# Three full score passes in place of two stacked passes and a pair of 33-row strips, in the third of four attentions

## The chip, the cores and the metric

The kernel runs on one core of one Trainium2 chip. The metric is the time of one execution on the device, in microseconds (us). TensorE, VectorE, ScalarE and GpSimd (PE, DVE, ACT and POOL in the profile) run side by side and wait for one another by semaphores; SyncE (SP) issues DMAs.

## The reference

Eight sequences of 256 tokens (2048 rows of 128) go through four layers, each a gated cross attention and a gated feed-forward part. The third attention (`_L2_xattn_ref`) has 8 heads, and its head split folds the sequences into the rows:

```python
def _split_heads(t):
    b, n, _ = t.shape
    t = t.reshape(b, n, HEADS, DIM_HEAD)
    return t.transpose(2, 0, 1, 3).reshape(HEADS, b * n, DIM_HEAD)
sim = jnp.einsum('hid,hjd->hij', qh, kh) * SCALE
mean = jnp.mean(sim, axis=-1, keepdims=True)
sim = (sim - mean) * ATTN_MATRIX_SCALE + mean
attn = jax.nn.softmax(sim, axis=-1)
out = jnp.einsum('hij,hjd->hid', attn, vh)
```

So every query meets all 2048 keys, in each of 8 heads. x has 128 features and the context has 96.

## The kernel before

The weights of queries and keys are folded into one 128 x 96 matrix for each head, so a query is a vector of 96 that is multiplied with the context itself. Numbers are split into two 16-bit halves, high and low, and a product of two split numbers is made of three 16-bit products: high by high, high by low, low by high. The context lies in `M.ct_hi` (97 rows, the 97th all ones) and `M.ct_lo` (96 rows), each with 2048 keys.

`attention_wide` works through 32 blocks (8 heads by 4 groups of 512 queries), each of 8 units of 256 keys. The order of the work is written out by hand, one list for each engine, and a wait on a semaphore stands ahead of each step. For block b and unit u (n = 8b + u) TensorE does:
- `max_scores(b + 2, 2u)` (L1245): scores in high halves alone, for a block two later, 512 keys at a time. Their row maximum is subtracted later. It writes the one bank MAXB, which VectorE's reduction (L1452, `largest`) has to have read.
- `scores(n + 2)` (L1272, L1273, L1277): the scores of a unit two later, keys on the partitions, 512 queries in each of two banks.
- `max_scores(b + 2, 2u + 1)`.
- `weighted(n)` (L1294, L1297): 16 products of p's halves with the context.
- at u = 1 `max_row(b + 1)` (L1255: turns the negated maxima into a row), at u = 2 `turn` (L1308), at u = 3 `query(b + 3)` (L1229 to L1231), at u = 5 `project` (L1316).

ScalarE does `exps(n + 2)`: the exponent twice, to `p` in 32 bits (L1368) and to its high half `p_hi` (L1370), and copies the high half of the query (L1354), the row of maxima (L1358), the first half of the sums (L1378). The low half `p_lo` = p - p_hi is made in two halves, one by VectorE (L1464) and one by GpSimd (L1416). VectorE's order in a unit is: reduction 2u (L1452), p_lo of unit n + 1 (L1464), reduction 2u + 1; at u = 0 ahead of these the second half of the sums (`u_second`, L1471), at u = 3 behind them the low half of the query (L1443), at u = 5 and 6 the addition to x (L1486), at u = 7 the maximum over keys (L1458). GpSimd does p_lo's other half, and at u = 0 a sum (L1424).

The products of the scores have 96 + 96 + 97 rows to be contracted, 289 together. Before, they are stacked: K1 and K2 hold 128 rows of keys each, K3 the last 32 and a row of ones, at partitions 0 and 64; S1, S2 and S3 hold the query rows that belong to them. The key stacks are made once, and the query stacks by five DMAs a block on SyncE's queue (`stack`, `double`). Two full passes with 128 rows each and a third with 33 rows make a bank's scores; the third ones of the two banks lie in different row groups of the array and run side by side.

Of the kernel before, what the change touches and what calls it, by code (L numbers as in the profile page):

```python
# [21 lines left out]
F16 = mybir.dt.float16  # L22
BF16 = mybir.dt.bfloat16
ALU = mybir.AluOpType
ACT = mybir.ActivationFunctionType
# [3 lines left out]
P = 128  # L29
D = 128  # L30
DC = 96
DA = DC + 1
NTOK = 2048
NT = NTOK // P
QB = 512
# [1097 lines left out]
def attention_wide(nc, M, layer):  # L1133
    L = LAYERS[layer]
    NB = L.H * NQ
    UQ = NT // 2
    NU = NB * UQ
    JOB, MAXB, UB = 6, 7, 4
    VW = DA + 1
    MAXS = NT  # L1140
    ps, A_hi, A_lo, C = M.ps, M.A_hi[layer], M.A_lo[layer], M.C[layer]

    with ExitStack() as ctx:
        def sb(name, shape, dt):
            return ctx.enter_context(nc.sbuf_tensor(f"aw_{name}", shape, dt))

        def sem(name):
            sems.append(nc.alloc_semaphore(f"aw_{name}"))
            return sems[-1]

        sems = []

        K1, K2, K3 = (sb(f"keys{i}", [P, NTOK], F16) for i in range(3))
        S1, S2, S3 = (sb(f"queries{i}", [P, 4, QB], F16) for i in range(3))
        QL = sb("q_lo", [DC, 2, QB], F16)
        p = sb("p", [P, 2, 2 * QB], F32)
        p_hi = sb("p_hi", [P, 3, 2 * QB], F16)
        p_lo = sb("p_lo", [P, 3, 2 * QB], F16)
# [4 lines left out]
        UT = sb("u_turned", [DC, 2, QB], F32)  # L1163
        rden = sb("rden", [P, 2, TQ, 1], F32)

        ones_set, keys_loaded = sem("ones_set"), sem("keys_loaded")
        q_ready, qhi_done, q_done = sem("q_ready"), sem("q_hi_done"), sem("q_lo_done")
        stacked = [sem(f"stacked{i}") for i in range(4)]
        doubled = [sem(f"doubled{i}") for i in range(4)]
        m_ready, m_done, n_done = sem("max_scores_ready"), sem("max_done"), sem("neg_max_done")  # L1170
        r_ready, r_done = sem("max_row_ready"), sem("max_row_done")
        st_ready, p_done, hi_done = sem("scores_ready"), sem("p_done"), sem("p_hi_done")
# [5 lines left out]
        def is_block(b):  # L1178
            return 0 <= b < NB

        def is_unit(n):
            return 0 <= n < NU

        with nc.Block() as block:
            @block.sync
            def _(sp):
                sp.dma_start(K1[0:DC, :], M.ct_hi[0:DC, :]).then_inc(keys_loaded, 16)
                sp.dma_start(K1[DC:P, :], M.ct_hi[0:32, :]).then_inc(keys_loaded, 16)
                sp.dma_start(K2[0:64, :], M.ct_hi[32:DC, :]).then_inc(keys_loaded, 16)
                sp.dma_start(K2[64:P, :], M.ct_lo[0:64, :]).then_inc(keys_loaded, 16)  # L1190
                for r in (0, 64):
                    sp.dma_start(K3[r:r + 32, :], M.ct_lo[64:DC, :]).then_inc(keys_loaded, 16)

                def stack(b):
                    c = b % 4
                    sp.wait_ge(qhi_done, b + 1)
                    sp.dma_start(S2[64:P, c, :], S1[0:64, c, :]).then_inc(stacked[c], 16)
                    sp.dma_start(S3[0:32, c, :], S1[64:DC, c, :]).then_inc(stacked[c], 16)
                    sp.wait_ge(q_done, b + 1)
                    sp.dma_start(S1[DC:P, c, :], QL[0:32, b % 2, :]).then_inc(stacked[c], 16)  # L1200
                    sp.dma_start(S2[0:64, c, :], QL[32:DC, b % 2, :]).then_inc(stacked[c], 16)

                def double(b):
                    c = b % 4
                    sp.wait_ge(stacked[c], 64 * (b // 4 + 1))
                    sp.wait_ge(r_done, b + 1)
                    sp.dma_start(S3[64:97, c, :], S3[0:33, c, :]).then_inc(doubled[c], 16)

                for b in range(3):
                    stack(b)  # L1210
                double(0)
                for b in range(NB):
                    if is_block(b + 1):
                        double(b + 1)
                    if is_block(b + 3):
                        stack(b + 3)

            @block.tensor
            def _(pe):
                def query(b):  # L1220
# [12 lines left out]
                def max_scores(b, k):  # L1233
                    t, kb = divmod(k, NQ)
                    if k == 0:
                        pe.wait_ge(qhi_done, b + 1)
                    step = MAXS * b + k
                    bank = MAXB
                    if b < 2:
                        bank = (UB + 1, MAXB)[k % 2]  # L1240
                        if step >= 2:
                            pe.wait_ge(m_done, step - 1)
                    else:
                        pe.wait_ge(m_done, step)
                    nc.tensor.matmul(ps[:, bank, :], S1[0:DC, b % 4, t * P:(t + 1) * P],  # L1245
                                     M.ct_hi[0:DC, kb * QB:(kb + 1) * QB], start=True, stop=True
                                     ).then_inc(m_ready, 1)

# [10 lines left out]
                def scores(n):  # L1259
                    b, u = divmod(n, UQ)  # L1260
                    c = b % 4
                    if n == 0:
                        pe.wait_ge(keys_loaded, 6 * 16)
                        pe.wait_ge(ones_set, 2)
                    if u == 0:
                        pe.wait_ge(stacked[c], 64 * (b // 4 + 1))
                        pe.wait_ge(doubled[c], 16 * (b // 4 + 1))
                    if n >= 2:
                        pe.wait_ge(hi_done, n - 1)
                    for i in range(2):  # L1270
                        o, ks = ps[:, 2 * (n % 2) + i, :], slice((2 * u + i) * P, (2 * u + i + 1) * P)
                        nc.tensor.matmul(o, K1[:, ks], S1[:, c, :], start=True, stop=False)  # L1272
                        nc.tensor.matmul(o, K2[:, ks], S2[:, c, :], start=False, stop=False)  # L1273
                    for i in range(2):
                        o, ks = ps[:, 2 * (n % 2) + i, :], slice((2 * u + i) * P, (2 * u + i + 1) * P)
                        rows = slice(64 * i, 64 * i + 33)
                        ins = nc.tensor.matmul(o, K3[rows, ks], S3[rows, c, :], start=False, stop=True)  # L1277
                    ins.then_inc(st_ready, 1)

                def weighted(n):  # L1280
# [48 lines left out]
                for b in range(NB):  # L1329
                    for u in range(UQ):  # L1330
                        n = UQ * b + u
# [19 lines left out]
            def _(act):  # L1351
                def query(b):
                    act.wait_ge(q_ready, b + 1)
                    nc.scalar.activation(S1[0:DC, b % 4, :], ps[0:DC, JOB, :], ACT.Copy).then_inc(qhi_done, 1)  # L1354

                def max_row(b):
                    act.wait_ge(r_ready, b + 1)
                    nc.scalar.activation(S3[32:33, b % 4, :], ps[0:1, JOB, :], ACT.Copy).then_inc(r_done, 1)  # L1358

                def exps(n):  # L1360
                    act.wait_ge(st_ready, n + 1)
# [26 lines left out]
                for b in range(3):  # L1388
                    query(b)
# [3 lines left out]
                for b in range(NB):  # L1393
                    for u in range(UQ):
                        n = UQ * b + u
# [11 lines left out]

            @block.gpsimd
            def _(pool):
                for r in (32, 96):  # L1410
                    nc.gpsimd.memset(K3[r:r + 1, :], 1.0).then_inc(ones_set, 1)

                def lows(n):
                    pool.wait_ge(hi_done, n + 1)
                    pool.wait_ge(p_done, n + 1)
                    nc.gpsimd.tensor_tensor(p_lo[:, n % 3, QB:], p[:, n % 2, QB:], p_hi[:, n % 3, QB:],  # L1416
                                            ALU.subtract).then_inc(lo_b, 1)

                def u_sum(b):
                    pool.wait_ge(ue_a, b + 1)  # L1420
                    pool.wait_ge(ue_b, b + 1)
                    if b >= 2:
                        pool.wait_ge(t_ready, b - 1)
                    nc.gpsimd.tensor_tensor(us[:, b % 2], UE[:, b % 2, :, 0:DC], UE[:, b % 2, :, VW:VW + DC], ALU.add  # L1424
                                            ).then_inc(us_done, 1)

                lows(0)
                for b in range(NB):
                    for u in range(UQ):
                        n = UQ * b + u  # L1430
                        if is_unit(n + 1):
                            lows(n + 1)
                        if u == 0 and is_block(b - 1):
                            u_sum(b - 1)
                u_sum(NB - 1)

            @block.vector
            def _(dve):
                def query(b):
                    dve.wait_ge(qhi_done, b + 1)  # L1440
                    if b >= 2:
                        dve.wait_ge(stacked[(b - 2) % 4], 64 * ((b - 2) // 4 + 1))
                    nc.vector.tensor_tensor(QL[:, b % 2, :], ps[0:DC, JOB, :], S1[0:DC, b % 4, :], ALU.subtract  # L1443
                                            ).then_inc(q_done, 1)

                def largest(b, k):
# [44 lines left out]
                for b in range(3):  # L1491
                    query(b)
# [5 lines left out]
                for b in range(NB):  # L1498
                    for u in range(UQ):
                        n = UQ * b + u  # L1500
# [707 lines left out]
```

## Time and profile before

| what | value |
|---|---|
| median of 3 runs | 2666.34 us (2664.91 to 2668.88) |
| the profiled execution's own time | 2664.91 us |
| its span, first to last instruction | 2662.8 us |
| mean granted TensorE clock | 0.922 |
| TensorE, VectorE, ScalarE, GpSimd busy | 2293.9, 1955.0, 1518.6, 517.3 us |
| third attention, first to last product starts | 1047.6 to 1896.9 us |

Busy time is the time in which an engine has an instruction under way. Products overlap in the pipeline: a product of 512 columns is shown 0.38 us long, and the next one starts 0.22 us after it. What a product costs its engine is read from start to start.

### The profile page before, as it was taken

To read this page: it belongs to the slowest core of one execution; us is meant where nothing else is said; L and a number is where in the kernel's file an instruction comes from. 1 tells how busy PE (TensorE), PEld (TensorE's weight loads), DVE (VectorE), ACT (ScalarE), POOL (GpSimd) and SP (SyncE) were. 2 spreads that over 40 slices of the span, in tenths; PEclk is the share of its full clock that TensorE was granted. 3 is DMA by queue.
4 is the path that set the end of the run, shared out by engine and by line. 5 is a ranking of instruction groups with operands and counts; after the bars stand their busy time and mean duration, and the time that the engine had idled before them with its cause. 6 is when DMAs were issued, how large, how long until landed. Compare 5 with 4: busy or idle time off the path is not lost. (4 is left out here: it accounts for less than half of the span.)

```text
span 2662.8 us, 53217 instructions
## 1 busy us (share of the span) xinstructions
PE 2293.9 (86%) x19264; PEld 1535.1 (58%) x19265; DVE 1955.0 (73%) x3972; ACT 1518.6 (57%) x2054; POOL 517.3 (19%) x451
## 2 busy tenths in 40 slices
PE   3699439999969996999999999999679959999777
PEld 3444227888746663455555555555456638888644
DVE  2566457888858886787787877877447758888778
ACT  1257206777635552566666666667468837777511
POOL 2100010000022221343443444444322110000000
PEclk9679669999979997899999999999789969999889
DMA  5001100000010001000000000000010000000000
GB/s 141 0 6 10 19 0 1 0 0 0 1 48 25 24 1 30 8 9 11 11 9 12 9 11 9 11 12 6 1 41 24 1 1 1 0 0 0 1 17 26
DMA packets 68181, 35.68 MB, mean 13 GB/s; under 512 B 40939, under 2 KB 63699, under 8 KB 67670
## 3 DMA queue, kind: packets, MB, share of 16 engines
q1 hardware_dynamic: 63412, 30.84, 4.8%
q10 hardware_dynamic: 4610, 2.71, 0.4%
q8 instruction: 101, 1.65, 0.2%
q14 instruction: 58, 0.48, 0.1%
HBM read 22.75 MB, written 2.10 MB: 9 GB/s over the span
## 5 line engine op out<-in xcount | busy, mean ns | idle before, releaser
L1368 ACT ACTIVATE aw_p<-ps 128x1024 f32<-128x1024 f32 x256 | 262.3, 1024 | 259.8 <-PE ps L1277 259.8
L1452 DVE TENSOR_REDUCE aw_max_part<-ps 128x1 f32<-128x512 f32 x512 | 349.8, 686 | 76.6 <-PE ps L1245 74.1
L1416 POOL TENSOR_TENSOR aw_p_lo<-aw_p,aw_p_hi 128x512 f16<-128x512 f32 x256 | 303.1, 1184 | 498.7 <-ACT aw_p_hi L1370 498.6
L1294 PE MATMUL ps<-ctx_hi_lo,aw_p_hi 128*128 128x194 f16 x2048 | 290.8, 247 | 1.1 <-DVE aw_p_lo L1464 0.7
L1464 DVE TENSOR_TENSOR aw_p_lo<-aw_p,aw_p_hi 128x512 f16<-128x512 f32 x256 | 267.3, 1044 | 22.4 <-ACT aw_p_hi L1370 22.4
L1297 PE MATMUL ps<-ctx_hi_lo,aw_p_lo 128*128 128x97 f16 x2048 | 279.4, 207 | 0.0
L1370 ACT ACTIVATE aw_p_hi<-ps 128x1024 f16<-128x1024 f32 x256 | 260.5, 1018 | 0.0
L428 POOL TENSOR_TENSOR ln_rstd<-ln_var_eps,neg_half 128x16 f32<-128x16 f32 x8 | 23.3, 2918 | 1129.3 <-DVE ln_var_eps L414 1094.8
L2095 DVE TENSOR_TENSOR ex_hidden_lo<-ex_hidden,ex_hidden_hi 128x512 f16<-128x512 f32 x256 | 195.3, 765 | 64.0 <-ACT ex_hidden L2052 63.7
L1245 PE MATMUL ps<-ctxT_hi,aw_queries 96*128 96x512 f16 x512 | 204.1, 400 | 35.8 <-DVE aw_max_part L1452 35.1
L1297 PEld LDWEIGHTS ps<-ctx_hi_lo,aw_p_lo 128*128 128x128 f16 x2048 | 200.3, 98 | 26.0
L2041 ACT ACTIVATE ex_silu<-ps 128x512 f32<-128x512 f32 x164 | 97.9, 597 | 191.6 <-PE ps L1981 189.3
L1977 PE MATMUL ps<-x_normT_hi,ex_w_hi 128*128 128x512 f16 x456 | 175.6, 385 | 34.6 <-POOL ex_w_lo L1942 34.3
L1294 PEld LDWEIGHTS ps<-ctx_hi_lo,aw_p_hi 128*128 128x128 f16 x2048 | 199.7, 97 | 4.8 <-issue 3.7
L1272 PE MATMUL ps<-aw_queries,aw_keys 128*128 128x512 f16 x512 | 194.9, 381 | 0.0
L1273 PE MATMUL ps<-aw_queries,aw_keys 128*128 128x512 f16 x512 | 194.4, 380 | 0.0
L2008 PE MATMUL ps<-ex_w_hi,ex_hidden_hi 128*128 128x128 f16 x1024 | 176.3, 220 | 20.3 <-DVE ex_hidden_lo L2095 16.6
L1010 ACT ACTIVATE at_p<-ps 128x1024 f32<-128x1024 f32 x128 | 131.1, 1024 | 102.6 <-PE ps L916 102.6
L1068 DVE TENSOR_REDUCE at_neg_max<-ps 128x2 f16<-128x512 f32 x256 | 174.3, 681 | 6.0 <-PE ps L895 5.6
L2104 DVE SCALAR_TENSOR_TENSOR x_res<-ps,comb,x_res 128x128 f32<-128x128 f32 x544 | 152.6, 343 | 35.5 <-PE ps L2012 30.1
L2012 PE MATMUL ps<-ex_w_hi,ex_hidden_lo 128*128 128x128 f16 x1024 | 176.3, 220 | 0.0
L2010 PE MATMUL ps<-ex_w_lo,ex_hidden_hi 128*128 128x128 f16 x1024 | 176.3, 220 | 0.0
(288 smaller groups left out, 5716.7 us busy)
## 6 DMA issues: line engine op xcount, KB each, us to landing
ex_w_raw<-in_L_w SPq DMA_DIRECT2D x8, 512.0 KB, 3.3
ex_w<-in_L_w SPq DMA_DIRECT2D x16, 256.0 KB, 2.8
aw_queries<-aw_queries SPq DMA_DIRECT2D x32, 64.0 KB, 2.0
aw_queries<-aw_q_lo SPq DMA_DIRECT2D x32, 64.0 KB, 2.0
ex_w_raw<-in_L_w SPq DMA_DIRECT2D x8, 256.0 KB, 2.6
raw<-in_L_q SPq DMA_DIRECT2D x3, 512.0 KB, 11.0
raw<-in_L_o SPq DMA_DIRECT2D x3, 512.0 KB, 12.8
raw<-in_L_k SPq DMA_DIRECT2D x3, 384.0 KB, 7.6
```

Of the source, the lines that this page charges most:

```text
L1245: nc.tensor.matmul(ps[:, bank, :], S1[0:DC, b % 4, t * P:(t + 1) * P], M.ct_hi[0:DC, kb * QB:(kb + 1) * QB], start=True, stop=True).then_i ...
L1272: nc.tensor.matmul(o, K1[:, ks], S1[:, c, :], start=True, stop=False)
L1273: nc.tensor.matmul(o, K2[:, ks], S2[:, c, :], start=False, stop=False)
L1294: nc.tensor.matmul(ps[:, bank, at:at + 2 * VW - 2], p_hi[:, n % 3, cols], M.cv[:, kt, 0:2 * VW - 2], start=kt == 0 and t % 2 == 0, stop=False,
L1297: ins = nc.tensor.matmul(ps[:, bank, at:at + DA], p_lo[:, n % 3, cols], M.cv[:, kt, 0:DA], start=False, stop=kt == NT - 1, skip_group_chec ...
L1368: nc.scalar.activation(p[:, n % 2, :].rearrange("p (b q) -> p b q", b=2), s, ACT.Exp, scale=1.0 / QS).then_inc(p_done, 1)
L1370: nc.scalar.activation(p_hi[:, n % 3, :].rearrange("p (b q) -> p b q", b=2), s, ACT.Exp, scale=1.0 / QS).then_inc(hi_done, 1)
L1416: nc.gpsimd.tensor_tensor(p_lo[:, n % 3, QB:], p[:, n % 2, QB:], p_hi[:, n % 3, QB:], ALU.subtract).then_inc(lo_b, 1)
L1452: nc.vector.tensor_reduce(mpart[:, b % 2, k:k + 1], ps[:, bank, :], AX.X, ALU.max).then_inc(m_done, 1)
L1464: nc.vector.tensor_tensor(p_lo[:, n % 3, 0:QB], p[:, n % 2, 0:QB], p_hi[:, n % 3, 0:QB], ALU.subtract).then_inc(lo_a, 1)
L2008: nc.tensor.matmul(o, hid_hi[b][:, f, tok], w2_hi[j][:, f, :], start=f == 0, stop=False)
L2095: nc.vector.tensor_tensor(hid_lo[q % 2][:, f, :], hid1[f % 2][:], hid_hi[q % 2][:, f, :], ALU.subtract).then_inc(hid_done, 1)
```

## The change

The stacks, the DMAs that fill them, the memsets and ten semaphores go. The scores read the context as it lies, and the query's halves from `q_hi` (97 rows: the 97th is the row of negated maxima, which ScalarE writes) and `q_lo` (96 rows), both with room for four blocks. A bank's scores are three passes: high keys with high queries (97 rows), low keys with high queries (96), high keys with low queries (96). So a unit has six products of 128 x 512 as before, but none of them run side by side.

```diff
-        K1, K2, K3 = (sb(f"keys{i}", [P, NTOK], F16) for i in range(3))
-        S1, S2, S3 = (sb(f"queries{i}", [P, 4, QB], F16) for i in range(3))
-        QL = sb("q_lo", [DC, 2, QB], F16)
+        q_hi = sb("q_hi", [DA, 4, QB], F16)
+        q_lo = sb("q_lo", [DC, 4, QB], F16)
...
-            @block.sync
-            def _(sp):
-                sp.dma_start(K1[0:DC, :], M.ct_hi[0:DC, :]).then_inc(keys_loaded, 16)
...
-                def stack(b):
-                    c = b % 4
-                    sp.wait_ge(qhi_done, b + 1)
-                    sp.dma_start(S2[64:P, c, :], S1[0:64, c, :]).then_inc(stacked[c], 16)
-                    sp.dma_start(S3[0:32, c, :], S1[64:DC, c, :]).then_inc(stacked[c], 16)
-                    sp.wait_ge(q_done, b + 1)
-                    sp.dma_start(S1[DC:P, c, :], QL[0:32, b % 2, :]).then_inc(stacked[c], 16)
-                    sp.dma_start(S2[0:64, c, :], QL[32:DC, b % 2, :]).then_inc(stacked[c], 16)
-
-                def double(b):
-                    c = b % 4
-                    sp.wait_ge(stacked[c], 64 * (b // 4 + 1))
-                    sp.wait_ge(r_done, b + 1)
-                    sp.dma_start(S3[64:97, c, :], S3[0:33, c, :]).then_inc(doubled[c], 16)
...
-                    if n == 0:
-                        pe.wait_ge(keys_loaded, 6 * 16)
-                        pe.wait_ge(ones_set, 2)
                     if u == 0:
-                        pe.wait_ge(stacked[c], 64 * (b // 4 + 1))
-                        pe.wait_ge(doubled[c], 16 * (b // 4 + 1))
+                        pe.wait_ge(q_done, b + 1)
+                        pe.wait_ge(r_done, b + 1)
                     if n >= 2:
                         pe.wait_ge(hi_done, n - 1)
                     for i in range(2):
                         o, ks = ps[:, 2 * (n % 2) + i, :], slice((2 * u + i) * P, (2 * u + i + 1) * P)
-                        nc.tensor.matmul(o, K1[:, ks], S1[:, c, :], start=True, stop=False)
-                        nc.tensor.matmul(o, K2[:, ks], S2[:, c, :], start=False, stop=False)
-                    for i in range(2):
-                        o, ks = ps[:, 2 * (n % 2) + i, :], slice((2 * u + i) * P, (2 * u + i + 1) * P)
-                        rows = slice(64 * i, 64 * i + 33)
-                        ins = nc.tensor.matmul(o, K3[rows, ks], S3[rows, c, :], start=False, stop=True)
+                        nc.tensor.matmul(o, M.ct_hi[:, ks], q_hi[:, c, :], start=True, stop=False)
+                        nc.tensor.matmul(o, M.ct_lo[:, ks], q_hi[0:DC, c, :], start=False, stop=False)
+                        ins = nc.tensor.matmul(o, M.ct_hi[0:DC, ks], q_lo[:, c, :], start=False, stop=True)
                     ins.then_inc(st_ready, 1)
...
-                    if b >= 2:
-                        dve.wait_ge(stacked[(b - 2) % 4], 64 * ((b - 2) // 4 + 1))
```

## Rows read from the trace of the kernel before

**Rows 1.** The page: busy time, share of the span and instructions of each engine.
```profile
PE 2293.9 (86%) x19264; PEld 1535.1 (58%) x19265; DVE 1955.0 (73%) x3972; ACT 1518.6 (57%) x2054; POOL 517.3 (19%) x451
```
**Rows 2.** Busy time by stretch: us, engines' busy us and instructions, granted clock, DMA.
```profile
1079.20:1084.00 4.80, 4.80 (x13) 1.20 (x12) 1.44 (x4) 1.94 (x2) 0.06 (x1) 0.52 0.00 0
1084.00:1887.60 803.60, 771.86 (x6624) 465.39 (x6623) 628.38 (x975) 553.48 (x630) 338.95 (x285) 1.00 0.04 10
```
**Rows 3.** Waits, 1300 to 1500 us: us in total, times, longest.
```profile
PE ps L1245 <- DVE aw_max_part L1452: 8.2, 16, 0.6
```
**Rows 4.** TensorE in order of time: start, length, instruction, idle before it.
```profile
1415.11 0.38 PE L1245 MATMUL ps<-ctxT_hi,aw_queries 96*128 96x512 f16 x1
1415.33 0.38 PE L1272 MATMUL ps<-aw_queries,aw_keys 128*128 128x512 f16 x1
...
1415.98 0.38 PE L1273 MATMUL ps<-aw_queries,aw_keys 128*128 128x512 f16 x1
1416.29 0.39 PE L1277 MATMUL ps<-aw_queries,aw_keys 33*128 33x512 f16 x2
1416.61 0.39 PE L1245 MATMUL ps<-ctxT_hi,aw_queries 96*128 96x512 f16 x1
...
1418.45 0.38 PE L1245 MATMUL ps<-ctxT_hi,aw_queries 96*128 96x512 f16 x1 [0.43 <-DVE aw_max_part L1452]
...
1424.02 0.38 PE L1255 MATMUL ps<-ident,aw_neg_max 128*1 128x128 f16 x4
1424.43 0.39 PE L1245 MATMUL ps<-ctxT_hi,aw_queries 96*128 96x512 f16 x1
```
**Rows 5.** TensorE around the query products of two blocks.
```profile
1405.05 0.38 PE L1231 MATMUL ps<-x_normT_hi,A_lo 128*96 128x512 f16 x1
1405.26 0.38 PE L1245 MATMUL ps<-ctxT_hi,aw_queries 96*128 96x512 f16 x1
...
1407.43 0.39 PE L1245 MATMUL ps<-ctxT_hi,aw_queries 96*128 96x512 f16 x1 [0.60 <-DVE aw_max_part L1452]
...
1430.80 0.38 PE L1231 MATMUL ps<-x_normT_hi,A_lo 128*96 128x512 f16 x1
```
**Rows 6.** VectorE in order of time, units u7 and u1.
```profile
1415.53 0.69 DVE L1452 TENSOR_REDUCE aw_max_part<-ps 128x1 f32<-128x512 f32 x1
1416.14 1.56 DVE L1464 TENSOR_TENSOR aw_p_lo<-aw_p,aw_p_hi 128x512 f16<-128x512 f32 x1
1417.62 0.68 DVE L1452 TENSOR_REDUCE aw_max_part<-ps 128x1 f32<-128x512 f32 x1
...
1422.21 1.56 DVE L1464 TENSOR_TENSOR aw_p_lo<-aw_p,aw_p_hi 128x512 f16<-128x512 f32 x1
1423.69 0.68 DVE L1452 TENSOR_REDUCE aw_max_part<-ps 128x1 f32<-128x512 f32 x1
```
**Rows 7.** GpSimd in order of time, the same units.
```profile
1416.00 1.16 POOL L1416 TENSOR_TENSOR aw_p_lo<-aw_p,aw_p_hi 128x512 f16<-128x512 f32 x1 [2.55 <-ACT aw_p_hi L1370]
...
1422.07 1.16 POOL L1416 TENSOR_TENSOR aw_p_lo<-aw_p,aw_p_hi 128x512 f16<-128x512 f32 x1 [0.89 <-ACT aw_p_hi L1370]
```
**Rows 8.** ScalarE in order of time, units u4, u6 and u7.
```profile
1405.46 0.59 ACT L1354 ACTIVATE aw_queries<-ps 96x512 f16<-96x512 f32 x1
...
1414.90 1.02 ACT L1370 ACTIVATE aw_p_hi<-ps 128x1024 f16<-128x1024 f32 x1
1416.72 1.02 ACT L1368 ACTIVATE aw_p<-ps 128x1024 f32<-128x1024 f32 x1 [0.80 <-PE ps L1277]
```
**Rows 9.** VectorE and GpSimd, released by the same copy, first p_lo of the stage.
```profile
1083.90 0.69 DVE L1464 TENSOR_TENSOR aw_p_lo<-aw_p,aw_p_hi 128x512 f16<-128x512 f32 x1 [3.33 <-ACT aw_p_hi L1370]
1083.94 1.66 POOL L1416 TENSOR_TENSOR aw_p_lo<-aw_p,aw_p_hi 128x512 f16<-128x512 f32 x1 [32.77 <-ACT aw_p_hi L1370]
```
**Rows 10.** ScalarE and VectorE at the start: the third query's copy and low half.
```profile
1054.93 0.59 ACT L1354 ACTIVATE aw_queries<-ps 96x512 f16<-96x512 f32 x1 [2.33 <-PE ps L1231]
...
1056.26 0.69 DVE L1443 TENSOR_TENSOR aw_q_lo<-ps,aw_queries 96x512 f16<-96x512 f32 x1 [2.94 <-DMA aw_queries<-aw_q_lo]
```

## What is predicted, and why

> **What bounds the kernel now.** I read the page first: TensorE is busy 86% of the span, more than any other engine [rows 1]. The change touches one stage only, so I then took the table by stretches. The third attention's steady part, 1084.0 to 1887.6 us, is 803.6 us in which TensorE is busy 771.9 us (96%) at granted clock 1.00; VectorE has 628.4, ScalarE 553.5 and GpSimd 339.0 [rows 2]. The chain of work that ended last names 2% of the span and helps nothing here, so I took the waits: in 200 us TensorE waits for VectorE's max reductions (L1452) 16 times, 8.2 us [rows 3]. Four per cent idle is little, but it sits always in the same places, and the change can move it.
>
> The next view is TensorE in order of time. One block (512 queries of one head, eight units of 256 keys) takes 25.75 us, by the same L1231 in two blocks (1405.05 and 1430.80) [rows 5]. Call the units u0 to u7. In a unit the order is first max product, scores, second max product, weighted sums. TensorE is back to back except at three places of a block:
> - second max product of u4 (1407.43): 0.60 idle, behind the query product's copy on ScalarE and its low half on VectorE [rows 5].
> - first max product of u0 (1418.45): 0.43 idle; by the steps of the weighted sums it would have come at about 1417.85 [rows 4].
> - first max product of u2 (1424.43): it comes 0.41 after the four L1255 products began, 0.74 after the reduction at 1423.69 began, as the one at 1407.43 comes 0.74 after its own [rows 4, 6]; the four products alone need about 0.31 (an estimate from the smallest such distance read in the stage), so about 0.1 is wait.
>
> Why is VectorE late there? At u7 its p_lo subtraction (L1464) takes 1.56 us where one alone takes 0.69 [rows 9], because GpSimd's half of the same work began 0.14 us before it (1416.00 against 1416.14) and runs until 1417.16. VectorE then ends 0.54 after GpSimd, at 1417.70; the reduction follows at 1417.62 (a VectorE instruction starts some 0.08 before the last one's end) and TensorE at 1418.45. At u1 it is the same: 1422.07 against 1422.21, 1.56 long, reduction at 1423.69 [rows 6, 7]. I counted 57 such collisions of 0.14 to 0.15 us among the 256 subtractions, two in nearly every block; the block of 25.75 repeats with a tick of 0.01. Where VectorE is first by 0.04 it takes 0.69 and GpSimd 1.66 instead of 1.16 [rows 9]. So who comes first decides, and the second waits.
>
> **TensorE's work.** Old scores of a unit: three steps of a full pass (1415.33 to 1415.98, 0.217 each), 0.31 to the pair of 33-row products, 0.32 from the pair to the next product, 1.28 together (1415.33 to 1416.61) [rows 4]. New: six full passes. The rows hold passes of 96 rows next to passes of 128 with the usual step (128 to 96: 1405.05 to 1405.26; 96 to 128: 1415.11 to 1415.33) [rows 4, 5], so 97 and 96 rows should step alike: 6 x 0.2165 = 1.30. The difference is +0.01 to +0.02 a unit; I take 0.015. So the pair, though it runs at once, cost 0.415 net of everything, nearly two passes: what its concurrency gains, the 0.095 ahead of it and the 0.105 behind it take away.
>
> The skill bears on both halves. The Trainium skill, "TensorEngine Tiling (Array Packing)", section Theoretical Speedup, promises up to 2x for contractions of at most 64 rows, and its Key Properties say that changing the tiling mode drains the engine. The trace agrees with both together: 0.31 and 0.32 around the pair instead of 0.22. By the first alone the pair would be worth one pass and the change would cost 0.2165 x 256 = 55 us; by row it is 4.
>
> **When scores are ready.** This term matters more. ScalarE's exponent starts 1.39 after the first score pass (1415.33 to 1416.72) [rows 4, 8]. New: 5 x 0.2165 to the start of the sixth pass and 0.42 to its reader (as 1415.11 to 1415.53) [rows 4, 6] = 1.50. So ScalarE, and behind it GpSimd (its subtraction starts 1.10 after L1370 does, 1414.90 to 1416.00 [rows 7, 8]), come 0.10 to 0.11 later against TensorE; I take 0.105. Most of it is hidden: weighted sums use these values two units later. It is not hidden where GpSimd's end holds VectorE and VectorE's reduction holds TensorE: u7 (scores of u6) and u1 (scores of u0).
>
> Walk a block from the query product Q (L1231 group) of u3. The wait at u4 starts from the query product and absorbs that unit's 0.015; ScalarE must be free for the copy (1405.46 [rows 8]); it would be 0.09 later and was free some 0.14 early (an estimate from back-to-back steps of 0.92 behind the exponent), so it stays free. u5 adds 0.015 until u6's scores start, then 0.105 through exponent, GpSimd, p_lo, reduction, first max of u0: +0.12 instead of +0.045. From there scores of u0 start, 0.105 again through GpSimd of u1 to the first max of u2; then u2 and u3 add 0.03: +0.135. A block: +0.255. TensorE's own 0.015 in u6, u7, u0, u1 vanishes in the two waits. Of 32 blocks 30 run beside max products, and the first of them settles in: 29 x 0.255 = +7.4 us. The last two blocks have no max products and TensorE sets their pace: 16 x 0.015 = +0.2, and the last exponent +0.1.
>
> **Does the collision keep its order?** Against TensorE, GpSimd comes 0.105 later and VectorE's p_lo (behind the unit's first max) 0.015. Its lead of 0.14 becomes 0.05. Observed: GpSimd ahead by 0.14 wins, VectorE ahead by 0.04 wins [rows 6, 7, 9]; 0.05 lies between. I take GpSimd first, since in both rows the earlier starter won.
> The Trainium skill, "SBUF — State Buffer", section SBUF: two separate sides, has it that whichever starts first keeps the shared port pair for its whole instruction. The trace agrees at both leads seen; by that rule 0.05 is enough and the sum stands.
>
> **What is removed elsewhere.** The DMAs: SyncE's queue only issued them; nobody but the first score pass and q_lo waited. In the steady state the waits of TensorE are those on VectorE [rows 3] and none for a DMA, so they give nothing; without that cover nothing is lost either, as q_done and r_done lie units before. The new waits for these stand ahead of a block's first scores, with the unit's second max and weighted sums queued behind. At the start VectorE's third q_lo waits 2.94 us for a DMA (1056.26) where its input was ready at about 1055.55 (copy 1054.93 plus 0.59, plus 0.04) [rows 10]: -0.7, handed on through the paced max products. There the first two units' scores run at a granted clock of 0.52 (1.2 GHz), 13 products in 4.8 us [rows 2]; a pass steps twice as long, and twelve passes take 12 x 0.43 = 5.1 against about 4.6 us as read: +0.5. Net -0.2 (bounds -0.7 and +0.1). The memsets (GpSimd) and ten fewer semaphores to clear lie where GpSimd has nothing to do: 0.
>
> **Sum.** 7.4 + 0.2 + 0.1 - 0.2 = +7.5 us on the profiled execution's 2664.91 (span 2662.8) = 2672.4. The median of before is 1.4 higher, 2666.34: so **2673.8 us**.
>
> **Rivals.**
> 1. VectorE gets the pair first at u7 (lead 0.05 not enough). Then p_lo of u7 takes 0.68, the u0 wait of 0.6 goes, and GpSimd ends 0.5 late. But the exponent of u7's scores is not earlier: it starts at Q+12.24 (Q the query product's start, by the steps above), and GpSimd's next subtraction 0.92 + 1.10 later, Q+14.26. VectorE's p_lo of u0 comes at Q+14.6 (weighted sums readable 13.50, u_second copy 0.51, reduction 0.60), so GpSimd is first, VectorE ends at 14.26 + 1.16 + 0.54 = 15.96, its second reduction starts at 15.89, and the first max of u1 0.74 later, Q+16.63. Before, that point was Q+16.57. The 0.55 gained is given back in the next unit; u1's collision then is 0.6 apart, the u2 wait goes, and the block ends at 25.77 against 25.75. Total about +0.5: 2666.8. For it: 0.05 is a third of the lead seen. Chance 0.27.
> 2. Faster: as 1, but u0 does not give it back. That needs VectorE's p_lo of u0 ahead of GpSimd's, which is 0.35 earlier there; from that point on 0.55 less 0.05 a block is kept: 29 x 0.5 = -14.5, 2652. Against it: both engines' starts hang on rows that don't move so far. Chance 0.06.
> 3. The 0.2 around the pair isn't a switch and stays with the neighbours: scores cost 6 x 0.2165 + 0.2, TensorE +0.215 x 256 = +55 less absorbed waits (1.3 a block, part of it): 2700 to 2722. Against: the plain passes on either side step 0.22. Chance 0.04.
> 4. GpSimd first, as forecast: 0.55. The rest, 0.08, is for what I don't see.
>
> **Numbers.** 0.2% is 5.3 us, about what a measurement of this kernel tells from no change. Case 4 lies at 2673.8 +- 3, five sixths of it beyond +5.3 us; case 1 within. Slower 0.54, same 0.37, faster 0.09. Range: from 2663 (case 1 less run spread of 2 and a start gain) to 2678 (+0.11 and +0.02 taken everywhere, 29 x 0.29, plus spread): 2663 to 2678; the likeliest case alone 2670.5 to 2677.
>
> **What would show it.** Score passes stepping 0.22 with 1.30 to the second max; exponent 1.50 behind the first pass; block 26.0 us (case 4) or 25.75 to 25.8 (case 1); p_lo of u7 and u1 still 1.56 with GpSimd 0.05 ahead, or 0.68 with GpSimd 1.66; waits of TensorE at u0 about 0.7 and at u2 0.2; no DMA wait at the start. Wrong if the 97-row and 96-row passes don't alternate at 0.22, if a 0.05 lead behaves otherwise, or if a later stage shifts by itself.

## The result

Eight runs of each kernel: 2674.98 us after (2671.06 to 2676.51) against 2667.82 us before (2664.91 to 2670.49), a ratio of 1.0026 with a 95% interval of 1.0016 to 1.0037. The change costs about 7.2 us (4.3 to 9.9 by the interval). The forecast was +7.5 us, a median of 2673.8 us. The median of the kernel before is 2667.82 over eight runs and was 2666.34 over the three that the forecast started from.

The page of the kernel after, busy time, share of the span and instructions (before: [rows 1]), and under it the table of its steady stretch (before: [rows 2]):

```profile
PE 2298.9 (86%) x19264; PEld 1578.0 (59%) x19265; DVE 1965.2 (74%) x3972; ACT 1516.2 (57%) x2054; POOL 512.5 (19%) x449
```
```profile
1084.00:1894.00 810.00, 776.87 (x6622) 506.87 (x6621) 636.59 (x971) 550.52 (x628) 336.22 (x284) 1.00 0.01 1
```

The numbers of instructions on PE are the same, so the form of a block is what has to be compared. Line numbers have moved: L1272 and L1273 are now L1232 and L1233, the 33-row L1277 is a full pass L1234, the max product L1245 is L1208, p_lo L1464 and L1416 are L1416 (DVE) and L1370 (POOL). TensorE after, in order of time, units u7, u0 and u1 (before: [rows 4]):

```profile
1413.64 0.38 PE L1208 MATMUL ps<-ctxT_hi,aw_q_hi 96*128 96x512 f16 x1
1413.86 0.38 PE L1232 MATMUL ps<-aw_q_hi,ctxT_hi 97*128 97x512 f16 x1
...
1414.95 0.38 PE L1234 MATMUL ps<-aw_q_lo,ctxT_hi 96*128 96x512 f16 x1
1415.17 0.38 PE L1208 MATMUL ps<-ctxT_hi,aw_q_hi 96*128 96x512 f16 x1
1417.08 0.38 PE L1208 MATMUL ps<-ctxT_hi,aw_q_hi 96*128 96x512 f16 x1 [0.52 <-DVE aw_max_part L1404]
...
1422.67 0.38 PE L1218 MATMUL ps<-ident,aw_neg_max 128*1 128x128 f16 x4
1423.17 0.39 PE L1208 MATMUL ps<-ctxT_hi,aw_q_hi 96*128 96x512 f16 x1
```

Six full passes take 1.31 (1413.86 to 1415.17), where the rows showed 1.28 before; over 240 units of each trace, start to start, the medians are 1.304 and 1.282. The step behind the second max product goes the other way: 0.215 after a stretch of full passes, 0.226 after the strips. A unit of TensorE's work has grown by 0.011 net. The wait at u0 is 0.52 and was 0.43; the one at u2 shows as 0.50 from the four L1218 products to the max product and was 0.41. VectorE and GpSimd in the same units (before: [rows 6, 7]):

```profile
1414.67 1.66 DVE L1416 TENSOR_TENSOR aw_p_lo<-aw_p,aw_p_hi 128x512 f16<-128x512 f32 x1
1416.25 0.68 DVE L1404 TENSOR_REDUCE aw_max_part<-ps 128x1 f32<-128x512 f32 x1
...
1420.85 1.66 DVE L1416 TENSOR_TENSOR aw_p_lo<-aw_p,aw_p_hi 128x512 f16<-128x512 f32 x1
1422.43 0.68 DVE L1404 TENSOR_REDUCE aw_max_part<-ps 128x1 f32<-128x512 f32 x1
```
```profile
1414.63 1.15 POOL L1370 TENSOR_TENSOR aw_p_lo<-aw_p,aw_p_hi 128x512 f16<-128x512 f32 x1 [2.56 <-ACT aw_p_hi L1327]
...
1420.81 1.15 POOL L1370 TENSOR_TENSOR aw_p_lo<-aw_p,aw_p_hi 128x512 f16<-128x512 f32 x1 [1.00 <-ACT aw_p_hi L1327]
```

GpSimd is first by 0.04 now and was by 0.14, and still has its 1.15 us undisturbed, while VectorE's 1.56 became 1.66. ScalarE's exponent follows the first pass by 1.51 (1413.86 to 1415.37 below) where it was 1.39 [rows 4, 8]; over the stage the medians are 1.50 and 1.39:

```profile
1415.37 1.02 ACT L1325 ACTIVATE aw_p<-ps 128x1024 f32<-128x1024 f32 x1 [0.81 <-PE ps L1234]
```

And the block, by the query product's third part in two blocks (before 25.75: [rows 5]), with the wait at u4 between:

```profile
1403.55 0.38 PE L1194 MATMUL ps<-x_normT_hi,A_lo 128*96 128x512 f16 x1
...
1405.94 0.39 PE L1208 MATMUL ps<-ctxT_hi,aw_q_hi 96*128 96x512 f16 x1 [0.48 <-DVE aw_max_part L1404]
...
1429.56 0.38 PE L1194 MATMUL ps<-x_normT_hi,A_lo 128*96 128x512 f16 x1
```

A block takes 26.01 us. The product at u4 comes 2.39 behind the query product's third part and came 2.38 behind it [rows 5], so that unit's part is absorbed, as the walk had it. The wait for the DMA at the start is gone, -0.71: first query product to first score pass is 31.87 us before (1047.56 to 1079.43) and 31.16 after (1042.96 to 1074.12).

**Where the profiled 6.2 us are** (2671.06 against 2664.91). The instruction L428 of each layer norm marks the stages. The third attention with the norm behind it, from its fifth to its sixth, is 868.3 us before (1035.5 to 1903.8) and 877.7 after (1030.9 to 1908.6), +9.4. Of these, 28 blocks from the first query product in the loop to the last are 720.41 and 727.52, +7.1; the start is +0.05 (the wait for the DMA -0.71; the twelve passes of the first two units, which run at half clock, +0.51, from 4.61 to 5.12; the first partial block +0.25); the units behind the last query product are +0.8. The last 1.4 belong to the clock: the last turn and projection took 0.64 and 1.16 us before, and 1.09 and 2.08 after, at a granted clock of 0.50 (1.2 GHz). Of the eleven profiles only this one of the kernel before has the projection at 1.16; in the other ten it takes 2.07 or 2.08, also in e4 and e8, which are built on the kernel before. The turn is 0.64 in e1, e3 and e8 and 0.96 to 1.09 in the others. So the projection's 0.9 us are scatter and not the change's; for the turn's 0.45 it stays open. Outside this stage the profiled run was 4.6 us ahead before it began and lost 1.4 behind it; the same instructions run there, and I come back to that scatter below.

### The profile page after: what moved, and what is told of

The parts are those of the page before. It is cut to its first block and busy times, and to the rows that moved or that the text cites. A ratio compares the mean times of both kernels' runs of the same rounds, so it can differ in the third digit from the quotient of the medians.

```text
span 2668.9 us, 52976 instructions
## 1 busy us (share of the span) xinstructions
PE 2298.9 (86%) x19264; PEld 1578.0 (59%) x19265; DVE 1965.2 (74%) x3972; ACT 1516.2 (57%) x2054; POOL 512.5 (19%) x449
## 2 busy tenths in 40 slices
DMA packets 58163, 26.97 MB, mean 10 GB/s; under 512 B 38443, under 2 KB 54003, under 8 KB 57654
## 3 DMA queue, kind: packets, MB, share of 16 engines
q8 instruction: 101, 1.65, 0.3%
## 5 line engine op out<-in xcount | busy, mean ns | idle before, releaser
L1370 POOL TENSOR_TENSOR aw_p_lo<-aw_p,aw_p_hi 128x512 f16<-128x512 f32 x256 | 302.3, 1181 | 511.6 <-ACT aw_p_hi L1327 511.4
L1416 DVE TENSOR_TENSOR aw_p_lo<-aw_p,aw_p_hi 128x512 f16<-128x512 f32 x256 | 280.5, 1096 | 23.1 <-ACT aw_p_hi L1327 23.1
L428 POOL TENSOR_TENSOR ln_rstd<-ln_var_eps,neg_half 128x16 f32<-128x16 f32 x8 | 23.3, 2916 | 1126.1 <-DVE ln_var_eps L414 1091.8
L1208 PE MATMUL ps<-ctxT_hi,aw_q_hi 96*128 96x512 f16 x512 | 201.6, 395 | 37.0 <-DVE aw_max_part L1404 33.8
L1232 PE MATMUL ps<-aw_q_hi,ctxT_hi 97*128 97x512 f16 x512 | 195.4, 382 | 0.0
L1233 PE MATMUL ps<-aw_q_hi,ctxT_lo 96*128 96x512 f16 x512 | 195.2, 381 | 0.0
L1234 PE MATMUL ps<-aw_q_lo,ctxT_hi 96*128 96x512 f16 x512 | 194.1, 379 | 0.0
```

Source lines behind the costliest of these rows:

```text
L1208: nc.tensor.matmul(ps[:, bank, :], q_hi[0:DC, b % 4, t * P:(t + 1) * P], M.ct_hi[0:DC, kb * QB:(kb + 1) * QB], start=True, stop=True).then ...
L1232: nc.tensor.matmul(o, M.ct_hi[:, ks], q_hi[:, c, :], start=True, stop=False)
L1233: nc.tensor.matmul(o, M.ct_lo[:, ks], q_hi[0:DC, c, :], start=False, stop=False)
L1416: nc.vector.tensor_tensor(p_lo[:, n % 3, 0:QB], p[:, n % 2, 0:QB], p_hi[:, n % 3, 0:QB], ALU.subtract).then_inc(lo_a, 1)
```

## The experiments

All are compared with the kernel before on the same chip; the ratio and its interval are to that kernel. "Block" is the period in the steady part, "stage" the distance between the same two norms' L428 in the profiled run.

| kernel | block us | stage us | median us | ratio to before, 95% interval |
|---|---|---|---|---|
| before | 25.75 | 868.3 | 2664 to 2668 in the sets | 1 |
| after | 26.01 | 877.7 | 2674.98 | 1.0026 (1.0016 to 1.0037) |
| e1 strips on plain halves | 25.785 | 872.5 | 2667.19 | 1.0010 (1.0001 to 1.0019) |
| e2 shorter exponent | 25.79 | 870.9 | 2667.70 | 1.0012 (1.0003 to 1.0020) |
| e3 VectorE first, changed kernel | 25.165 | 852.6 | 2650.67 | 0.9946 (0.9933 to 0.9959) |
| e4 VectorE first, kernel before | 25.09 | 850.6 | 2644.58 | 0.9922 (0.9907 to 0.9938) |
| e5 VectorE first at u7 | 25.75 | 870.2 | 2666.80 | 1.0004 (0.9994 to 1.0015) |
| e6 VectorE first at u7, u0 | 25.165 | 853.6 | 2650.38 | 0.9939 (0.9925 to 0.9952) |
| e7 strips one after the other | 26.97 | 912.1 | 2710.15 | 1.0169 (1.0151 to 1.0187) |
| e8 both moves, kernel before | 24.43 | 830.5 | 2627.93 | 0.9852 (0.9838 to 0.9865) |
| e9 both moves, changed kernel | 24.51 | 833.9 | 2632.40 | 0.9860 (0.9842 to 0.9878) |

**e1: strips without stacks and DMAs.** Did the stacks and their DMAs cost the old kernel anything, or is its time that of its order of passes?

```diff
-                        ins = nc.tensor.matmul(o, M.ct_hi[0:DC, ks], q_lo[:, c, :], start=False, stop=True)
+                    for i in range(2):
+                        o, ks = ps[:, 2 * (n % 2) + i, :], slice((2 * u + i) * P, (2 * u + i + 1) * P)
+                        rows = slice(64 * i, 64 * i + 33)
+                        ins = nc.tensor.matmul(o, M.ct_hi[rows, ks], q_hi[rows, c, :], start=False, stop=True)
```

> The changed kernel, but each bank's third pass is a 33-row strip again (rows 0 to 32 and 64 to 96 of the plain halves, side by side), without stacks and DMAs; this leaves out most of the third product's rows and adds others. Theory A (the time comes from TensorE's order of passes and from when the scores are ready, nothing from the DMAs): block 25.75 us, time that of the kernel before, less up to 0.7 at the start: 0 to -1 us. Rival B (the stacks' DMAs, or 128 rows against 97, cost the old kernel something in the steady state): the block is shorter than 25.75 and the time below before by more than 3 us.

The block is 25.785, within 0.03 of before's: the steps around the pair are the old 0.31 and 0.32, the wait at u0 the old 0.6, and no DMA runs. So the DMAs cost the old steady state nothing, and rival B fell. The rows account for the 0.03: the second and third steps between e1's full passes are 0.218 and 0.218 where the kernel before has 0.215 and 0.215, 0.007 a unit by the medians (1.289 against 1.282). The walk of the prediction has five units on the path (u5, u6, u0, u2, u3), which makes 0.035. Why the steps differ no run shows. The time is 2.7 us above before (interval 0.3 to 5), where 0 to -1 was expected: a miss. In the profiled run the loop has 0.9 us more than before. The stretch from the first query product to the loop has 2.2 more (50.9 us against 48.7 in both other kernels); its last 15 us (1077.6 to 1092.6) had a granted clock of 0.75, where the kernel before had 1.00 from 1084.0 on [rows 2]. Behind the last query product there are 1.1 more, 0.9 of them in the same projection at half clock. So some 3 of the 4.2 us by which the stage is longer are the clock's in this one profile; whether the other runs share it stays open.

**e2: the exponent shortened by what the scores come late.** The test that tells readiness from pass time:

```diff
-                    nc.scalar.activation(p[:, n % 2, :].rearrange("p (b q) -> p b q", b=2), s, ACT.Exp,
+                    w = QB if n < 2 else QB - 64
+                    nc.scalar.activation(p[:, n % 2, :].rearrange("p (b q) -> p b q", b=2)[:, :, 0:w], s[:, :, 0:w],
+                                         ACT.Exp, scale=1.0 / QS).then_inc(p_done, 1)
```

> The changed kernel with ScalarE's first exponent over 448 instead of 512 columns of each bank from the third unit on (it leaves out an eighth of p): some 0.107 us shorter, so GpSimd's subtraction begins again when it did before, while TensorE's six passes stay. Theory A (late readiness of the scores, through ScalarE, GpSimd, VectorE, holds TensorE at u0 and u2): block 26.01 - 2 x 0.107 = 25.80, GpSimd 0.15 ahead at u7 and u1 again, time about 6 us below the changed kernel, 1 to 2 above before. Rival C (TensorE's longer score passes are the cost; ScalarE is idle a third of the time): no change, block 26.0, 7 us above before.

TensorE's passes are those of the changed kernel, and ScalarE has 0.10 us less to do (its first exponent is 0.92 long where it was 1.02). Query products stand at 1403.69 and 1429.48. GpSimd, VectorE and TensorE in turn:

```profile
1415.09 1.15 POOL L1371 TENSOR_TENSOR aw_p_lo<-aw_p,aw_p_hi 128x512 f16<-128x512 f32 x1 [2.56 <-ACT aw_p_hi L1328]
```
```profile
1415.24 1.55 DVE L1417 TENSOR_TENSOR aw_p_lo<-aw_p,aw_p_hi 128x512 f16<-128x512 f32 x1
1416.72 0.68 DVE L1405 TENSOR_REDUCE aw_max_part<-ps 128x1 f32<-128x512 f32 x1
...
```
```profile
1403.69 0.38 PE L1192 MATMUL ps<-x_normT_hi,A_hi 128*96 128x512 f16 x1
...
1429.48 0.38 PE L1192 MATMUL ps<-x_normT_hi,A_hi 128*96 128x512 f16 x1
```

The lead is 0.15 again, VectorE's subtraction 1.55, the block 25.79. Of the 0.255 that the change adds to a block, 0.22 are late readiness on an engine that is idle a third of the time, and 0.04 TensorE's own. Rival C fell.

**e3 and e4: VectorE's half always first.** One wait in GpSimd's list, on the changed kernel and on the one before:

```diff
                     pool.wait_ge(p_done, n + 1)
+                    pool.wait_ge(lo_a, n + 1)
                     nc.gpsimd.tensor_tensor(p_lo[:, n % 3, QB:], p[:, n % 2, QB:], p_hi[:, n % 3, QB:],
```

> The changed kernel with one more wait: GpSimd's half of each p_lo starts only when VectorE's half is done. Theory A: the 1.66 us subtractions at u7 and u1 become 0.68, TensorE's waits at u0 (0.69) and u2 (0.18) go, only that at u4 (0.64) stays: block 25.15, 25 us below the changed kernel, 18 below before. Rival 1 of the prediction in its general form (the gain is given back in the next unit, since the exponents are no earlier): block 25.7 to 25.8, about the time of before. Rival D (GpSimd's half now comes too late for the weighted sums): slower than the changed kernel.

> The kernel before with the same one wait. Theory A: block 25.75 - 0.60 - 0.10 = 25.05 us, some 20 us below before; against the same wait on the changed kernel only TensorE's own difference of 8 x 0.0125 = 0.1 a block is left, 3 us instead of 7. Rival C (the difference of 7 us is TensorE's passes): the two stay 7 us apart.

VectorE, GpSimd and TensorE of e3 at u7 and u0:

```profile
1432.55 0.68 DVE L1417 TENSOR_TENSOR aw_p_lo<-aw_p,aw_p_hi 128x512 f16<-128x512 f32 x1
1433.46 0.69 DVE L1405 TENSOR_REDUCE aw_max_part<-ps 128x1 f32<-128x512 f32 x1 [0.23 <-PE ps L1208]
```
```profile
1433.40 1.16 POOL L1371 TENSOR_TENSOR aw_p_lo<-aw_p,aw_p_hi 128x512 f16<-128x512 f32 x1 [1.29 <-DVE aw_p_lo L1417]
```
```profile
1434.30 0.38 PE L1208 MATMUL ps<-ctxT_hi,aw_q_hi 96*128 96x512 f16 x1
```

The subtraction takes 0.68, the reduction waits for TensorE and no more the other way, and the first max product of u0 has no wait. Blocks are 25.165 and 25.09, as expected within 0.04, so neither is the gain given back nor does GpSimd's half come too late. The blocks differ by 0.075, where 8 x 0.0125 = 0.1 was expected, and the two stages by 2.0 us. Their medians differ by 6, and I put no weight on that: e4's six runs fall into three at 2641.1 to 2642.0, with a mean granted clock of 0.922 to 0.924, and three at 2647.2 to 2647.4, with 0.918 to 0.920. Against the kernel before, e3 is 14 us faster and e4 20, by the medians. Against the kernel that each is built on, the added wait saved about 21 us both times, an estimate from the ratios (1.0026 to 0.9946, and 1 to 0.9922).

**e5 and e6: VectorE first in single units.** The same wait, under `if n % UQ == 0` (u7's) and `if n % UQ in (0, 1)` (u7's and u0's), on the changed kernel. e5 is rival 1 of the prediction, built.

> The changed kernel, GpSimd waiting for VectorE's half only for the p_lo made in u7. Theory A with the prediction's rival 1 as a mechanism: at u0 the first max product comes without a wait, but GpSimd's next subtraction is then ahead of VectorE's (about 0.35), VectorE ends late and the first max product of u1 waits some 0.6; the wait at u2 goes. Block 25.79, 6 us below the changed kernel, about 0 to 1 above before. Theory E (a collision avoided is a collision saved): 0.7 a block kept, block 25.3, 20 us below the changed kernel.

> The same at u7 and at u0. Theory A: now nothing gives the gain back, since u1's collision is behind enough slack: block 25.17 as with the wait everywhere, 24 us below the changed kernel, 16 below before. If the collisions of the other units matter too: block between 25.2 and 25.8.

e5's VectorE, GpSimd and TensorE, from u7 to u1; its query product began at 1425.30:

```profile
1436.84 0.68 DVE L1418 TENSOR_TENSOR aw_p_lo<-aw_p,aw_p_hi 128x512 f16<-128x512 f32 x1
...
1439.85 1.41 DVE L1418 TENSOR_TENSOR aw_p_lo<-aw_p,aw_p_hi 128x512 f16<-128x512 f32 x1
1441.18 0.68 DVE L1406 TENSOR_REDUCE aw_max_part<-ps 128x1 f32<-128x512 f32 x1
```
```profile
1437.69 1.16 POOL L1372 TENSOR_TENSOR aw_p_lo<-aw_p,aw_p_hi 128x512 f16<-128x512 f32 x1 [3.45 <-DVE aw_p_lo L1418]
1439.56 1.16 POOL L1372 TENSOR_TENSOR aw_p_lo<-aw_p,aw_p_hi 128x512 f16<-128x512 f32 x1 [0.70 <-ACT aw_p_hi L1327]
```
```profile
1438.60 0.38 PE L1208 MATMUL ps<-ctxT_hi,aw_q_hi 96*128 96x512 f16 x1
...
1441.92 0.39 PE L1208 MATMUL ps<-ctxT_hi,aw_q_hi 96*128 96x512 f16 x1 [0.41 <-DVE aw_max_part L1406]
```

The wait at u0 is gone (1438.60 is 13.30 behind the query product, 13.96 in the changed kernel). In the next unit GpSimd is first by 0.29, VectorE's subtraction takes 1.41, and u1's max product comes at 16.62 with a new wait: the prediction's rival had 14.26 for GpSimd's start (it is 14.26) and 16.63 for the product. So 0.66 is gained at u0, 0.58 given back at u1 and 0.18 saved at u2: 25.75 a block, the old time (25.79 was expected). e6 stops the giving back with u0's wait and has the 25.165 of e3. Only these two units matter: leaving the other six as they were costs nothing.

**e7: strips that can't run side by side.** e1 with `rows = slice(0, 33)` for both.

> The kernel of e1 with both strips on rows 0 to 32, so they can't run side by side (it leaves out most of the third product's rows). Theory A (0.31 ahead of the pair and 0.32 behind it are what a change of the row group's size costs, and running side by side saves one pass): the second strip steps 0.22 behind the first, scores take 1.28 + 0.22 = 1.50, seven of a block's eight units show it (u4 absorbs it): block 25.79 + 7 x 0.2165 = 27.30 us, some 48 us above before, 41 above the changed kernel. Rival F (the distances belong to 33-row products as such, each of which costs more than a full pass): scores 1.6 us or more, block 28 or more.

TensorE of e7:

```profile
1401.34 0.38 PE L1233 MATMUL ps<-aw_q_hi,ctxT_lo 96*128 96x512 f16 x1
1401.66 0.60 PE L1237 MATMUL ps<-aw_q_hi,ctxT_hi 33*128 33x512 f16 x2
1402.19 0.39 PE L1208 MATMUL ps<-ctxT_hi,aw_q_hi 96*128 96x512 f16 x1
```

Before the pair 0.32 as ever, behind it 0.53 where it was 0.32 [rows 4], the two strips together 0.60 long where they were 0.39. So running side by side was worth 0.21, one pass. The second strip starts 0.226 behind the first and the next product 0.308 behind that (medians), so the two distances around the strips cost 0.095 and 0.09 over a full pass whether the strips run side by side or not, and rival F fell. The block is 26.97 and not 27.30: I had let the wait at u0 stand at 0.6, but the reduction that ends it hangs on the unit's first max product, so a later second one only eats the wait (0.41 from last weighted sum to max product where it was 0.62, and none at u2).

**e8 and e9: the third wait too.** With GpSimd behind VectorE, VectorE's low half of the query goes behind the second reduction of u4:

```diff
-                        if u == 3 and is_block(b + 3):
+                        if u == 4 and is_block(b + 3):
                             query(b + 3)
```

> The kernel before with GpSimd behind VectorE everywhere, and VectorE's low half of the query (the third wait, u4) moved from u3 to behind the second reduction of u4. Theory A: the last of TensorE's three waits goes, block 25.09 - 0.66 = 24.43, 38 us below before. If a new wait takes its place (the query's bank, the turned sums): block above 24.6.

> The changed kernel with both moves. Theory A: block 25.17 - 0.64 = 24.52, all of TensorE's steps back to back; 0.09 a block or 3 us above the other one, which is then what six full passes cost by themselves.

Both stretches from 1300 to 1500 us, e8 and then e9; TensorE is busy 200.00 of 200, where the kernel before has 191.6:

```profile
1300.00:1500.00 200.00, 200.00 (x1734) 122.23 (x1733) 149.65 (x265) 144.48 (x165) 82.98 (x75) 1.00 0.04 11
```
```profile
1300.00:1500.00 200.00, 200.00 (x1725) 132.34 (x1724) 149.68 (x264) 142.43 (x163) 82.26 (x74) 1.00 0.01 1
```

The blocks are 24.43 and 24.51, within 0.01 of what was expected. e8 beats both kernels: 1.5% below before, 39 us. The change by itself then costs 0.08 a block, 2.2 us over 28 blocks of the loop. The medians differ by 4.5 us, but the two intervals overlap for the most part, so that difference says nothing more.

## Why the prediction was right

- **TensorE's passes**, +0.015 a unit: from the first score pass to the second max product it is +0.022 (1.304 against 1.282), and the step behind that product, which the prediction did not look at, gives 0.011 back. Net 0.011 a unit, and 0.08 a block where nothing hides it (e9 against e8). That 0.015 lies between the two is luck.
- **Readiness**, +0.105: measured 0.11 (medians 1.50 against 1.39), and e2 takes it back and the block with it. It was the larger part of the sum, 0.22 of 0.255 a block.
- **The block**: 26.01 where 25.75 + 0.255 was forecast. The places, too: the first max product of u0 comes 0.12 later after the query product (13.96 against 13.84), that of u2 0.23 later. Against e3, where neither waits, the changed kernel's waits are 0.66 at u0 and 0.18 at u2; about 0.7 and 0.2 were forecast.
- **The collision**: a lead of 0.04 to 0.05 was enough for GpSimd in all 58 collisions with such a lead that I counted in the profile, VectorE's subtraction 1.66 each time. As VectorE wins when it is ahead by 0.04 to 0.05 (same trace, 13 times, its 0.69 against GpSimd's 1.66), the order is that of the starts down to 0.04. The Trainium skill, "SBUF — State Buffer", section SBUF: two separate sides, says that the one that starts first keeps the shared pair for its whole instruction; this trace agrees at both leads.
- **Number of blocks**: 29 was about one short of what the trace has: 28 in the loop are 7.11, the first partial one 0.25 and the last, up to its last max product, 0.39; together 7.75 where 7.4 was forecast. The two blocks without max products, where no later step gives anything back, cost 0.35 (0.2 was forecast), the last exponent 0.1 as forecast.
- **DMAs and start**: nothing in the steady state (e1); at the start -0.71 and +0.51, net -0.20 as forecast.
- **Rival 1**, the return of the gain: not what happened in the changed kernel, but e5 shows that it is what would have happened. **Rival 2** is e6 and e3: without the giving back the block is 0.585 shorter than before's, 0.84 shorter than the changed kernel's; I had said 0.5 against before, as I left the wait at u2 (0.09) where it was. **Rival 3**: wrong, the plain passes step 0.22 on both sides; what the pair's side-by-side run is worth is measured by e7.
- **The total** fits better than it should, and that is luck. The profiled run's own +6.2 is a sum of +9.4 in the stage and -3.2 outside it; of the 9.4 the change explains 8.0 (7.5 was forecast) and the clock at the stage's end 1.4. The interval of the medians, 4.3 to 9.9 us, would have held a sum of 5 or of 9 as well; what bears the account is the block.

The Trainium skill's "TensorEngine Tiling (Array Packing)", section Key Properties, says that changing the tiling mode drains the engine. e1 and e7 agree: 0.31 and 0.32 around the strips, and 0.31 on both sides when they run one after the other. They show the distances; that it is a drain is the page's word.

## What to carry over

Where a saturated engine waits in the same few places of every period, walk the period once: what a change costs is what it does to the chain that ends in those waits, and an engine that is idle a third of the time can own most of it. Running two strips side by side in different row groups was worth one pass (0.21 us) here but paid 0.2 us for the change of form on both sides, so it should need more than one pair at a time to win by much (an estimate from these numbers; no run has two pairs in a row). Two engines of which the later one has to wait for the earlier, as VectorE and GpSimd here, should be given an order by a semaphore where one of them is on the path: a wait added to GpSimd saved 0.66 a block at the collision, and only when the next unit's collision was ordered too was it kept.

## What was not expected of the hardware

- Identical instructions outside the changed stage took different times from kernel to kernel. The stretch from the first norm's L428 to the second's, with the first attention in it, took 204.4 us before (95.16 to 299.53) and 200.7 after (94.76 to 295.46), and between 200.0 and 206.6 in the experiments. The mean granted clock there is below 1 and not the same, 0.83 and 0.85. The table by stretch, 90 to 290 us, before and then after:

```profile
90.00:290.00 200.00, 166.33 (x1397) 77.66 (x1398) 118.05 (x231) 109.34 (x144) 8.81 (x3) 0.83 0.11 12
```
```profile
90.00:290.00 200.00, 166.78 (x1424) 80.52 (x1424) 119.92 (x232) 109.24 (x144) 8.80 (x3) 0.85 0.11 12
```

  So one profiled pair can hide or feign half of an effect of 7 us. The period of a block repeats to 0.01 us and is the safer measure.
- The same turn and projection at the stage's end took 1.8 us in one profile and 3.2 in the other, after equal pauses of TensorE ahead of them (1.65 and 0.68). The granted clock from 1896 to 1900 us was 0.95 before, and from 1899 to 1902 us 0.50 after. TensorE at that end, before and then after:

```profile
1895.58 0.64 PE L1308 MATMUL ps<-ident,aw_u_sum 128*96 128x128 f32 x4 [1.65 <-POOL aw_u_sum L1424]
1896.91 1.16 PE L1316 MATMUL ps<-C,aw_u_turned 96*128 96x128 f32 x8 [0.68 <-ACT aw_u_turned L1386]
```
```profile
1898.99 1.09 PE L1265 MATMUL ps<-ident,aw_u_sum 128*96 128x128 f32 x4 [1.65 <-POOL aw_u_sum L1378]
1900.76 2.08 PE L1273 MATMUL ps<-C,aw_u_turned 96*128 96x128 f32 x8 [0.68 <-ACT aw_u_turned L1343]
```
